# Attention in steps of a whole block: sixteen half groups of scores mixed with maxima, then the block's sixteen pairs of products, into one output bank

## The chip, the cores and the metric

The kernel runs on one core of one Trainium2 chip. The metric is the device time of one execution in microseconds (us), the median of several runs.

## What is computed

One transformer block with modulation, on x of 2 x 2048 x 576 in float32, 16 heads of 36 columns:

```python
ada = silu(c) @ W_ada + b_ada
shift_msa, scale_msa, gate_msa, shift_mlp, scale_mlp, gate_mlp = split(ada, 6)
h = modulate(layernorm(x), shift_msa, scale_msa)
x = x + gate_msa * attention(h, W_qkv, b_qkv, W_proj, b_proj)
h = modulate(layernorm(x), shift_mlp, scale_mlp)
x = x + gate_mlp * (gelu(h @ W_fc1 + b_fc1) @ W_fc2 + b_fc2)
# attention, for each of 2 x 16 (batch, head): softmax(q k^T / 6) v over 2048 keys, then @ W_proj
```

## The kernel before

The program has four stages one after the other: `phase_qkv`, `phase_attention`, `phase_proj`, `phase_mlp`. Each engine has its own instruction list, written out by hand, and the lists are tied together by semaphores; nothing reorders them. The change is in `phase_attention` and in the last chunk of `phase_qkv`.

**Attention.** There are 32 (batch, head) pairs, called heads here. For each head two things are computed from queries and keys.

- *Maxima.* TensorE multiplies 128 queries by 512 keys into one PSUM bank `sp` (`score_max`, L1024), and VectorE reduces the bank to the maximum of each row (L1083). A head has 64 of these units. When a head's 64 are there, VectorE takes the maxima of four (L1089), TensorE transposes the result (L1030), VectorE splits it into two parts `mh` and `ml` (L1095, L1097), and SyncE writes them as two further rows into the head's query tile, so that the scores of the next pass have the maximum already subtracted.
- *Probabilities and values.* For each half group x (128 keys by 512 queries) TensorE computes scores into one of three PSUM banks `st` (`scores_t`, L1042) and ScalarE takes the exponential into half of a tile `pt` (`exps`, L1132; 8 tiles). Two half groups make a group. For a group (`products`, L1053) TensorE multiplies both halves of the probabilities by the values, one to partitions 0 to 36 and one to partitions 64 to 100 of an output bank `op`; the trace has four matmul records for a group. Eight groups make a block (512 queries by all keys): their products accumulate in one bank. ScalarE then moves the two halves of the bank out (L1143 to `oa`, L1144 to `ob`), GpSimd adds them (L1197), SyncE stores the sum. There are 4 blocks in a head and 128 in all.

**The order.** `plan` is a list of 258 steps. Step b holds the 8 half groups 8b to 8b+7, 8 maxima units that run 72 ahead (`THERE = 72`: the first 72 are made in `phase_qkv`), and after them the products of the four groups of step b - 1. Within a step TensorE takes the units in turn: maximum, scores, maximum, scores, and so on; in place 2 there is no maximum, and the last maximum follows the last scores. A matmul to an `sp` bank waits until the bank's use three units earlier has been reduced (`slot_free`; three banks `sp`). A matmul of scores waits until the exponential three half groups earlier has been read (`s_p`, x - 2). There are two output banks `op`; the products of a block wait until the block before last has been moved out (`s_oa`).

ScalarE does, in a step, the 8 exponentials, and in every second step behind them both evictions of a finished block. So a step is a run of 16 matmuls for scores and maxima (called the score run below) and a run of products (the product run), in turn. Banks: 3 `st`, 2 `op`, 3 `sp`.

The last 9 steps with scores have no maxima left. From step `LAST` = 248 on, five steps also have a *turn*: one matmul into an `sp` bank (L1061), a VectorE product (L1123) and a ScalarE copy (L1152), for the stage behind. The projection's weights (`weight`, `W0`), the row sums (`INV`) and first tokens are loaded in between at given steps.

**The last chunk of `phase_qkv`.** TensorE computes nine feature tiles (14 matmuls each, L595), each evicted by ScalarE (L820, L821). `maxima(c, kind, n)` puts two maxima units of head 1 ahead of each of the last four tiles (L574, reduced at L744). Head 1's queries and keys are loaded before that (`second_loads`, L477).

Of the kernel before, what the change touches and what calls it, by code (L numbers as in the profile page):

```python
# [9 lines left out]
ALU = mybir.AluOpType  # L10
# [13 lines left out]
NCH = T // CH  # L24
# [265 lines left out]
def phase_qkv(nc, A, ident, adaT, eps, bq, sc, qs0, ks0, qs1, ks1, hh0, lo0, mx, nm, mh, ml, gd, xf, cond, W_ada,  # L290
# [96 lines left out]
    def maxima(c, kind, n):  # L387


        place = n + 4 if kind == "qk" else n  # L390
        k = 26 * (c - HCH) + 2 * place - 18
        if 0 <= k < 64:
            return range(k, k + 2)
        if c == NCH - 1 and place > 8:
            return range(64 + 2 * (place - 9), 66 + 2 * (place - 9))
        return range(0)

    def evacuated(e, n):
# [455 lines left out]
def phase_attention(nc, A, W, ident, qs0, ks0, qs1, ks1, mx, nm, mh, ml, gd, W_proj, b_proj, xf, qkh, qkl, vd, ot,  # L854
# [9 lines left out]
    NB = 3  # L864
    NP = 8
    G = NH * 32
    NBAT = G // 4
    NBLK = G // 8
    W0 = 24
    LAST = NBAT - 8  # L870
    INV = NBLK // 2 + 6
    THERE = 72
    qs = [qs0, qs1, A.sb("qs2", [128, L], R)]
    ks = [ks0, ks1, A.sb("ks2", [128, L], R)]
    vs = [A.sb(f"vs{i}", [128, 16, VW]) for i in range(2)]
# [2 lines left out]
    ob = [A.sb(f"ob{i}", [VW, 512]) for i in range(2)]  # L878
    oc = W.oc
    st = [A.ps(f"st{i}", [128, 512]) for i in range(3)]  # L880
    op = [A.ps(f"op{i}", [128, 512]) for i in range(2)]
    sp = [A.ps(f"sp{i}", [128, 512]) for i in range(3)]
    s_qk, s_m, s_v, s_o = A.sems("qk", NB), A.sems("m", NB), A.sems("v", 2), W.s_o
    s_one = A.sem("one")
    s_s, s_mx, s_nm, s_mt, s_mh = A.sem("s"), A.sem("mx"), A.sem("nm"), A.sem("mt"), A.sem("mh")
# [5 lines left out]

    plan, slots = [], []
    todo = THERE
    for b in range(NBAT + 2):
        s = Step()
        s.b, s.last = b, None
        s.late = plan[-1].last if plan else None
        s.slot = None
        if s.late is not None:
            s.slot = len(slots)  # L900
            slots.append(("mh", s.late))
        s.units = [[] for _ in range(9)]
        for i in range(min(8, NH * 64 - todo)):
            s.units[(0, 1, 3, 4, 5, 6, 7, 8)[i]].append((todo, len(slots)))
            slots.append(("mx", todo))
            todo += 1
            if todo % 64 == 0:
                s.last = todo // 64 - 1
        s.turn = s.turn_slot = None
        if LAST < b <= LAST + KT:  # L910
            s.turn, s.turn_slot = b - LAST - 1, len(slots)
            slots.append(("turn", s.turn))
        s.now = b - 1 if 0 < b <= NBAT else None
        s.block = (b - 3) // 2 if b > 2 and b % 2 else None
        plan.append(s)

    def slot_free(e, k):

        if k > 2:
            kind, n = slots[k - 3]  # L920
            if kind == "mx":
                e.wait_ge(s_mx, n - THERE + 1)
            elif kind == "turn":
                e.wait_ge(W.s_u, n + 1)
            else:
                e.wait_ge(s_mh, 2 * n)
# [8 lines left out]

    def weight(b):

        j, r = divmod(b - W0, 4)
        return divmod(j, KT) if 0 <= j < 2 * KT and r == 0 else (None, None)

    def sync(e):
# [28 lines left out]
        for s in plan:  # L970
            i, kt = weight(s.b)
            if i is not None:
                if i == 1 and kt < 2:
                    e.wait_ge(W.w[0].lo, KT)
                W.w[i].load(e, kt, W.stg, W_proj)
            if s.late is not None:
                max_rows(s.late)
            if s.b < NBAT:
                h, r = divmod(s.b, 8)
                if r == 0 and h + 2 < NH:  # L980
                    load(h + 2)
                if r == 2 and h + 1 < NH:
                    load_v(h + 1)
            if s.block is not None:
                h, u = divmod(s.block, 4)
                hd, i = h % H, s.block % 2
                cols = slice((h // H) * L + u * 512, (h // H) * L + u * 512 + 512)
                e.wait_ge(s_oc, s.block + 1)
                e.dma_start(ot[hd * D:hd * D + D, cols], oc[i][0:D, :]).then_inc(s_o[i], 16)
                e.dma_start(sm[hd:hd + 1, cols], oc[i][D:D + 1, :]).then_inc(s_o[i], 16)  # L990
                if s.block == INV - 4:
                    for i in range(2):
                        e.wait_ge(s_o[i], 32 * NBLK // 4)
                    W.load_sums(e, 0, sm)
                elif s.block == INV + 4:
                    for c in range(HCH):
                        W.place(e, 0, c)
            if s.b == LAST - 2:
                W.load_tokens(e, 0, W.oi, ot)
            elif s.b == LAST + 1:  # L1000
                e.wait_ge(W.s_sel, 5)
                W.load_x(e, 0, W.x1, xf)
# [15 lines left out]
    def tensor(e):  # L1018
        def score_max(n, slot):
            h, k = divmod(n, 64)  # L1020
            qb, k4, i = k // 4, k % 4, h % NB
            loaded(e, h)
            slot_free(e, slot)
            e.matmul(sp[slot % 3][:, :], qs[i][0:108, qb * 128:qb * 128 + 128], ks[i][0:108, k4 * 512:k4 * 512 + 512],  # L1024
                     start=True, stop=True).then_inc(s_s, 1)

        def max_rows(h, slot):
            e.wait_ge(s_nm, h)
            slot_free(e, slot)
            e.transpose(sp[slot % 3][0:16, 0:128], nm[:, :], ident[:, :]).then_inc(s_mt, 1)  # L1030

        def scores_t(x):
            h, u, kb = x // 64, (x // 16) % 4, x % 16
# [11 lines left out]
        def products(g):  # L1045
            h, blk, j = g // 32, g // 8, g % 8
            if g % 32 == 0:
                e.wait_ge(s_v[h % 2], 16 * (h // 2 + 1))
            if j == 0 and blk > 1:
                e.wait_ge(s_oa, 2 * (blk - 1))  # L1050
            e.wait_ge(s_p, 2 * g + 2)
            for a in range(2):
                ins = e.matmul(op[blk % 2][64 * a:64 * a + VW, :], vs[h % 2][:, 2 * j + a, :],  # L1053
                               pt[g % NP][:, a * 512:a * 512 + 512], start=j == 0, stop=j == 7)
            ins.then_inc(s_pv, 1)

        def turn(kt, slot):
            e.wait_ge(W.s_sel, 5)
            e.wait_ge(W.s_rr, 32 * HCH)
            slot_free(e, slot)  # L1060
            e.matmul(sp[slot % 3][:, :], W.sel[:, kt, :], W.rr[:, 0, :], start=True, stop=True).then_inc(W.s_ta, 1)  # L1061

        for s in plan:
            if s.late is not None:
                max_rows(s.late, s.slot)
            for q in range(9):
                for n, slot in s.units[q]:
                    score_max(n, slot)
                if q < 8 and s.b < NBAT:
                    scores_t(8 * s.b + q)  # L1070
            if s.turn is not None:
                turn(s.turn, s.turn_slot)
            if s.now is not None:
                for q in range(4):
                    products(4 * s.now + q)

    def vector(e):
        def score_max(n, slot):
            k = n % 64
            e.wait_ge(s_s, n - THERE + 1)  # L1080
            if k < 2:
                e.wait_ge(s_nm, n // 64 - 1)
            e.tensor_reduce(mx[:, k // 4, k % 4:k % 4 + 1], sp[slot % 3][:, :], AX.X, ALU.max).then_inc(s_mx, 1)  # L1083

        def row_max(h):
            e.wait_ge(s_mx, 64 * (h + 1) - THERE)
# [4 lines left out]
        def max_rows(h, slot):  # L1091
            e.wait_ge(s_mt, h)
            rows_there(e, h - 1)
            src = sp[slot % 3][0:16, 0:128]
            e.tensor_copy(mh[:, :], src).then_inc(s_mh, 1)  # L1095
            e.wait_ge(s_mh, 2 * h - 1)
            e.tensor_tensor(ml[:, :], src, mh[:, :].bitcast(F), ALU.subtract).then_inc(s_mh, 1)  # L1097
# [10 lines left out]
        for s in plan:  # L1108
            if s.late is not None:
                max_rows(s.late, s.slot)  # L1110
            for q in range(9):
                for n, slot in s.units[q]:
                    score_max(n, slot)
                    if n % 64 == 63:
                        row_max(n // 64)
            if s.block == INV:
                W.invert(e, 0)
            if s.b == LAST:
# [1 line left out]
            if s.turn is not None:  # L1120
                e.wait_ge(W.s_ta, s.turn + 1)
                e.wait_ge(W.s_a[0], 48)
                e.tensor_tensor(W.oi[:, s.turn, :], sp[s.turn_slot % 3][:, :], W.oi[:, s.turn, :], ALU.mult).then_inc(  # L1123
                    W.s_u, 1)

    def scalar(e):
        def exps(x):
# [3 lines left out]
                e.wait_ge(s_pv, g - NP + 1)  # L1131
            e.activation(pt[g % NP][:, a * 512:a * 512 + 512], st[x % 3][:, :], ACT.Exp, scale=SCALE).then_inc(s_p, 1)  # L1132

        for s in plan:
            if s.b < NBAT:
                for q in range(8):
                    exps(8 * s.b + q)
            if s.block is not None:
                i = s.block % 2
                e.wait_ge(s_pv, 8 * (s.block + 1))  # L1140
                if s.block > 1:
                    e.wait_ge(s_oc, s.block - 1)
                e.activation(oa[i][:, :], op[i][64:64 + VW, :], ACT.Copy).then_inc(s_oa, 1)  # L1143
                e.activation(ob[i][:, :], op[i][0:VW, :], ACT.Copy).then_inc(s_oa, 1)  # L1144
            if s.block == INV + 1:
                W.high(e, 0)
            i, kt = weight(s.b - 2)
# [702 lines left out]
```

## Time and profile before

| what | us |
|---|---|
| median of 3 runs | 3583.03 (3578.46 to 3584.28) |
| the profiled execution, its own time | 3576.74 |
| its span, first to last instruction | 3574.8 |
| attention, first matmul to end of the last | 458.37 to about 2443.7 |
| TensorE busy by the records | 3506.8 (98%) |
| VectorE busy | 1885.4 (53%) |
| ScalarE busy | 1557.3 (44%) |
| GpSimd busy | 360.5 (10%) |

The ends of matmul records are modelled, and records overlap, so 98% does not say that TensorE has no gaps; the starts of weight loads (rows of PEld) and of matmuls say more. PE is TensorE, PEld its weight loads, DVE VectorE, ACT ScalarE, POOL GpSimd, SPq the queue of SyncE. A row of the timeline merges instructions of one line: start, time from the first's start to the last's end, engine, line, operation, tiles, count, and in brackets the idle time before it with what ended it.

### The profile page before, as it was taken

The page shows a single profiled execution, that of the slowest core. Times are in us where ns is not written, and L with a number is a line of the kernel's source. Part 1 is how long each engine was busy: PE and PEld are TensorE (multiplying, and loading weights), DVE is VectorE, ACT ScalarE, POOL GpSimd, SP SyncE. Part 2 cuts the span into 40 slices and gives each one's busy share as a digit, 9 for nine tenths or more (in the row PEclk, how much of TensorE's full clock was granted, in tenths as well). Part 3 has the DMA queues.
Part 4 walks back from the last instruction along what each step waited for, and adds up shares of the span by engine and source line. Part 5 has one row for each costly group of instructions (what it writes and reads, how often), then busy time and mean ns, then how long its engine had stood idle before and what let it go on. Part 6 is the DMA issues. An engine that isn't in the chain of part 4 may idle for free. (4 is left out here: it accounts for less than half of the span.)

```text
span 3574.8 us, 46332 instructions
## 1 busy us (share of the span) xinstructions
PE 3506.8 (98%) x16996; PEld 2252.1 (63%) x16996; DVE 1885.4 (53%) x3415; ACT 1557.3 (44%) x2904; POOL 360.5 (10%) x284
## 2 busy tenths in 40 slices
PE   7999999999999999999999999999889999999999
PEld 5888844444444444444444444436779899898988
DVE  5446566666666666666666666634552322333232
ACT  3223256566655655565556555665550111211010
POOL 1000010111100000000000000014521010000000
PEclk9999999999999999999999999999999999999999
DMA  5554431211212111111212111114763132422221
GB/s 193 163 172 142 136 84 29 58 44 41 53 30 52 29 48 33 40 43 32 52 29 53 29 49 33 29 37 136 261 204 106 61 100 65 142 83 93 73 87 50
DMA packets 144672, 285.54 MB, mean 80 GB/s; under 512 B 18290, under 2 KB 44146, under 8 KB 137536
## 3 DMA queue, kind: packets, MB, share of 16 engines
q1 hardware_dynamic: 143236, 282.57, 25.8%
q8 instruction: 142, 2.33, 0.3%
q14 instruction: 78, 0.64, 0.1%
q10 hardware_dynamic: 1216, 0.00, 0.0%
HBM read 177.09 MB, written 104.34 MB: 79 GB/s over the span
## 5 line engine op out<-in xcount | busy, mean ns | idle before, releaser
L1083 DVE TENSOR_REDUCE q_mx<-b_sp 128x1 f32<-128x512 f32 x1976 | 1203.9, 681 | 614.1 <-PE b_sp L1024 614.1
L1132 ACT ACTIVATE b_pt<-b_st 128x512 f32<-128x512 f32 x2048 | 1030.9, 626 | 782.4 <-PE b_st L1042 782.3
L1053 PE MATMUL b_op<-b_pt,b_vs 128*37 128x512 f32 x4096 | 929.5, 596 | 0.0
L1053 PEld LDWEIGHTS b_op<-b_pt,b_vs 128*37 128x37 f32 x4096 | 223.8, 114 | 537.1 <-issue 458.1
L1805 ACT ACTIVATE d_af<-n_pf,q_mx 128x512 f32<-128x512 f32 x144 | 98.9, 687 | 730.3 <-PE n_pf L1728 729.5
L1745 PE MATMUL d_pm<-d_vl,d_ah 128*128 128x288 f32 x1152 | 339.9, 295 | 0.0
L1746 PE MATMUL d_pm<-d_vh,d_al 128*128 128x288 f32 x1152 | 339.8, 295 | 0.0
L1744 PE MATMUL d_pm<-d_vh,d_ah 128*128 128x288 f32 x1152 | 339.7, 295 | 0.0
L1197 POOL TENSOR_TENSOR w_oc<-b_oa,b_ob 37x512 f32<-37x512 f32 x128 | 161.3, 1260 | 1721.7 <-ACT b_ob L1144 1712.2
L1024 PE MATMUL b_sp<-q_hh,q_lo 108*128 108x512 f32 x696 | 295.6, 425 | 4.5 <-PEq L846 4.5
L1042 PE MATMUL b_st<-q_lo,q_hh 110*128 110x512 f32 x704 | 275.3, 414 | 1.8 <-ACT b_pt L1132 1.8
L1042 PE MATMUL b_st<-q_qs,q_ks 110*128 110x512 f32 x704 | 273.2, 409 | 0.2 <-ACT b_pt L1132 0.2
L1024 PE MATMUL b_sp<-q_ks,q_qs 108*128 108x512 f32 x640 | 271.7, 424 | 0.0
L1024 PE MATMUL b_sp<-b_ks,b_qs 108*128 108x512 f32 x640 | 270.2, 422 | 0.0
L1042 PE MATMUL b_st<-b_qs,b_ks 110*128 110x512 f32 x640 | 246.6, 406 | 0.0
L1744 PEld LDWEIGHTS d_pm<-d_vh,d_ah 128*128 128x128 f32 x1152 | 216.4, 188 | 0.7
L1745 PEld LDWEIGHTS d_pm<-d_vl,d_ah 128*128 128x128 f32 x1152 | 216.4, 188 | 0.7
L1746 PEld LDWEIGHTS d_pm<-d_vh,d_al 128*128 128x128 f32 x1152 | 216.4, 188 | 0.0
L1766 DVE CAST d_ah<-d_af 128x512 fp32r<-128x512 f32 x144 | 61.5, 427 | 280.3 <-ACT d_af L1805 280.3
L1024 PEld LDWEIGHTS b_sp<-q_hh,q_lo 108*128 108x128 f32 x696 | 131.7, 189 | 104.4 <-issue 88.3
L1779 DVE TENSOR_TENSOR d_ug<-d_pm,d_gt 128x288 f32<-128x288 f32 x128 | 58.5, 457 | 250.8 <-PE d_pm L1746 250.8
L1042 PEld LDWEIGHTS b_st<-q_lo,q_hh 110*128 110x128 f32 x704 | 131.9, 188 | 86.6 <-ACT b_pt L1132 67.9
(299 smaller groups left out, 4599.7 us busy)
## 6 DMA issues: line engine op xcount, KB each, us to landing
qkh<-a_th SPq DMA_DIRECT2D x72, 256.0 KB, 2.0
qkl<-a_tl SPq DMA_DIRECT2D x72, 256.0 KB, 2.2
d_yi<-y SPq DMA_DIRECT2D x64, 288.0 KB, 3.0
vd<-a_vx SPq DMA_DIRECT2D x8, 1184.0 KB, 6.2
b_vs<-vd SPq DMA_DIRECT2D x32, 296.0 KB, 2.8
a_x<-in_x SPq DMA_DIRECT2D x8, 1152.0 KB, 6.7
ot<-w_oc SPq DMA_DIRECT2D x128, 72.0 KB
y<-d_yi SPq DMA_DIRECT2D x32, 288.0 KB, 2.2
```

The costliest lines, as they stand in the source:

```text
L1024: e.matmul(sp[slot % 3][:, :], qs[i][0:108, qb * 128:qb * 128 + 128], ks[i][0:108, k4 * 512:k4 * 512 + 512], start=True, stop=True).then_i ...
L1042: e.matmul(st[x % 3][:, :], ks[i][0:110, kb * 128:kb * 128 + 128], qs[i][0:110, u * 512:u * 512 + 512], start=True, stop=True).then_inc(s_ ...
L1053: ins = e.matmul(op[blk % 2][64 * a:64 * a + VW, :], vs[h % 2][:, 2 * j + a, :], pt[g % NP][:, a * 512:a * 512 + 512], start=j == 0, stop= ...
L1083: e.tensor_reduce(mx[:, k // 4, k % 4:k % 4 + 1], sp[slot % 3][:, :], AX.X, ALU.max).then_inc(s_mx, 1)
L1132: e.activation(pt[g % NP][:, a * 512:a * 512 + 512], st[x % 3][:, :], ACT.Exp, scale=SCALE).then_inc(s_p, 1)
L1197: e.tensor_tensor(oc[i][:, :], oa[i][:, :], ob[i][:, :], ALU.add).then_inc(s_oc, 1)
L1744: e.matmul(out, ah[:, f, ts], vh[:, f, cs], start=f == 0, stop=False)
L1745: e.matmul(out, ah[:, f, ts], vl[:, f, cs], start=False, stop=False)
L1746: ins = e.matmul(out, al[:, f, ts], vh[:, f, cs], start=False, stop=f == NT - 1)
L1766: e.tensor_copy(ah[:, f, :], af[m % 2][:, :]).then_inc(s_ah, 1)
L1779: e.tensor_tensor(ug[m % 2][:, :], pm[m % 4][:, 0:HALF], gt[:, b, cs], ALU.mult).then_inc(s_ug, 1)
L1805: e.activation(af[m % 2][:, :], pf[m % 4][:, :], ACT.Gelu_apprx_tanh, bias=b1[:, half * NT + f:half * NT + f + 1]).then_inc(s_af, 1)
```

## The change

Steps become whole blocks. For the first 124 blocks (`LAST = NBLK - 4`) step b holds the 16 half groups of block b, each scores matmul directly behind a maximum (16 maxima while there are any), and then the products of the same block's 8 groups. There are four banks `sp` and one bank `op`: a use of an `sp` bank waits for the use four units earlier, and a block's first product waits until the block before it has been moved out. ScalarE moves out the half at partition 64 at the start of the next step, ahead of its first exponential, and the other half behind that step's exponential 12 (counted from 0). The last four blocks go in steps of 8 half groups with the products of the 4 groups before, one step later than their scores; in these steps both evictions stand ahead of the exponentials. 80 maxima units instead of 72 are made in `phase_qkv`: two ahead of each of the last eight feature tiles. The loads, the weights and the turn keep about their places.

```diff
@@ phase_qkv, maxima
-        if c == NCH - 1 and place > 8:
-            return range(64 + 2 * (place - 9), 66 + 2 * (place - 9))
+        if c == NCH - 1 and place > 4:
+            return range(64 + 2 * (place - 5), 66 + 2 * (place - 5))
@@ phase_attention
-    NBAT = G // 4
     NBLK = G // 8
-    W0 = 24
-    LAST = NBAT - 8
+    W0 = 12
+    LAST = NBLK - 4
     INV = NBLK // 2 + 6
-    THERE = 72
+    THERE = 80
...
-    op = [A.ps(f"op{i}", [128, 512]) for i in range(2)]
-    sp = [A.ps(f"sp{i}", [128, 512]) for i in range(3)]
+    op = A.ps("op", [128, 512])
+    sp = [A.ps(f"sp{i}", [128, 512]) for i in range(4)]
...
-    for b in range(NBAT + 2):
+    for b in range(NBLK + 6):
         s = Step()
-        s.b, s.last = b, None
+        s.b, k = b, b - LAST
         s.late = plan[-1].last if plan else None
-        s.slot = None
+        s.slot = s.last = s.turn = s.turn_slot = None
...
-        s.units = [[] for _ in range(9)]
-        for i in range(min(8, NH * 64 - todo)):
-            s.units[(0, 1, 3, 4, 5, 6, 7, 8)[i]].append((todo, len(slots)))
-            slots.append(("mx", todo))
-            todo += 1
-            if todo % 64 == 0:
-                s.last = todo // 64 - 1
-        s.turn = s.turn_slot = None
-        if LAST < b <= LAST + KT:
-            s.turn, s.turn_slot = b - LAST - 1, len(slots)
+        if k < 0:
+            s.halves, s.groups, s.block = range(16 * b, 16 * b + 16), range(8 * b, 8 * b + 8), b - 1 if b else None
+        else:
+            x = 16 * LAST + 8 * k
+            s.halves = range(x, min(x + 8, 2 * G))
+            s.groups = range(x // 2 - 4, min(x // 2, G)) if k else range(0)
+            s.block = LAST - 1 + k // 2 if k == 0 or k > 2 and k % 2 else None
+        s.units = []
+        for x in s.halves:
+            if todo < NH * 64:
+                s.units.append((todo, len(slots)))
+                slots.append(("mx", todo))
+                todo += 1
+                if todo % 64 == 0:
+                    s.last = todo // 64 - 1
+        if 0 < k <= KT:
+            s.turn, s.turn_slot = k - 1, len(slots)
             slots.append(("turn", s.turn))
-        s.now = b - 1 if 0 < b <= NBAT else None
-        s.block = (b - 3) // 2 if b > 2 and b % 2 else None
...
-        if k > 2:
-            kind, n = slots[k - 3]
+        if k > 3:
+            kind, n = slots[k - 4]
...
-        j, r = divmod(b - W0, 4)
+        j, r = divmod(b - W0, 2)
@@ sync
-            if s.b < NBAT:
-                h, r = divmod(s.b, 8)
+            if s.b < LAST:
+                h, r = divmod(s.b, 4)
                 if r == 0 and h + 2 < NH:
                     load(h + 2)
-                if r == 2 and h + 1 < NH:
+                if r == 1:
                     load_v(h + 1)
@@ tensor
-            if j == 0 and blk > 1:
-                e.wait_ge(s_oa, 2 * (blk - 1))
+            if j == 0 and blk:
+                e.wait_ge(s_oa, 2 * blk)
             e.wait_ge(s_p, 2 * g + 2)
             for a in range(2):
-                ins = e.matmul(op[blk % 2][64 * a:64 * a + VW, :], vs[h % 2][:, 2 * j + a, :],
+                ins = e.matmul(op[64 * a:64 * a + VW, :], vs[h % 2][:, 2 * j + a, :],
...
-            for q in range(9):
-                for n, slot in s.units[q]:
+            for q, x in enumerate(s.halves):
+                for n, slot in s.units[q:q + 1]:
                     score_max(n, slot)
-                if q < 8 and s.b < NBAT:
-                    scores_t(8 * s.b + q)
+                scores_t(x)
             if s.turn is not None:
                 turn(s.turn, s.turn_slot)
-            if s.now is not None:
-                for q in range(4):
-                    products(4 * s.now + q)
+            for g in s.groups:
+                products(g)
@@ scalar
+        def evict(block, half):
+            i = block % 2
+            e.wait_ge(s_pv, 8 * (block + 1))
+            if block > 1:
+                e.wait_ge(s_oc, block - 1)
+            to, r = ((oa[i], 64), (ob[i], 0))[half]
+            e.activation(to[:, :], op[r:r + VW, :], ACT.Copy).then_inc(s_oa, 1)
+
         for s in plan:
-            if s.b < NBAT:
-                for q in range(8):
-                    exps(8 * s.b + q)
             if s.block is not None:
-                i = s.block % 2
-                e.wait_ge(s_pv, 8 * (s.block + 1))
-                if s.block > 1:
-                    e.wait_ge(s_oc, s.block - 1)
-                e.activation(oa[i][:, :], op[i][64:64 + VW, :], ACT.Copy).then_inc(s_oa, 1)
-                e.activation(ob[i][:, :], op[i][0:VW, :], ACT.Copy).then_inc(s_oa, 1)
+                evict(s.block, 0)
+                if s.b >= LAST:
+                    evict(s.block, 1)
+            for q, x in enumerate(s.halves):
+                exps(x)
+                if q == 12 and s.block is not None:
+                    evict(s.block, 1)
```

## Rows read from the trace of the kernel before

**Rows 1.** The profile's page: span and clock, and busy time by engine
```profile
span 3574.8 us, 46332 instructions
PE 3506.8 (98%) x16996; PEld 2252.1 (63%) x16996; DVE 1885.4 (53%) x3415; ACT 1557.3 (44%) x2904; POOL 360.5 (10%) x284
...
PEclk9999999999999999999999999999999999999999
```
**Rows 2.** Busy time in stretches: us, PE, PEld, DVE, ACT, POOL, PEclk, DMA share, GB/s
```profile
480.00:1000.00 520.00, 520.00 (x2154) 242.13 (x2154) 332.19 (x560) 315.55 (x614) 70.64 (x54) 1.00 0.17 43
...
2000.00:2360.00 360.00, 360.00 (x1491) 167.63 (x1488) 229.27 (x387) 213.22 (x416) 28.98 (x23) 1.00 0.14 36
```
**Rows 3.** Timeline of one usual step and the next step's start
```profile
1519.80 0.49 PE L1024 MATMUL b_sp<-q_ks,q_qs 108*128 108x512 f32 x1
...
1520.33 4.88 DVE L1083 TENSOR_REDUCE q_mx<-b_sp 128x1 f32<-128x512 f32 x8 [2.85 <-PE b_sp L1024]
...
1520.57 4.03 ACT L1132 ACTIVATE b_pt<-b_st 128x512 f32<-128x512 f32 x8 [3.71 <-PE b_st L1042]
...
1523.53 0.19 PEld L1024 LDWEIGHTS b_sp<-q_ks,q_qs 108*128 108x128 f32 x1 [0.17 <-issue]
...
1523.96 0.15 PEld L1053 LDWEIGHTS b_op<-b_pt,b_vs 128*37 128x37 f32 x4 [0.25 <-issue]
...
1527.53 0.50 PE L1024 MATMUL b_sp<-q_ks,q_qs 108*128 108x512 f32 x1
```
**Rows 4.** Timeline, the two steps that open attention
```profile
458.37 0.47 PE L1024 MATMUL b_sp<-q_hh,q_lo 108*128 108x512 f32 x1 [4.55 <-PEq L846]
...
461.86 7.92 DVE L1083 TENSOR_REDUCE q_mx<-b_sp 128x1 f32<-128x512 f32 x13 [0.16 <-PE b_sp L1024]
...
468.05 0.19 PEld L1024 LDWEIGHTS b_sp<-q_hh,q_lo 108*128 108x128 f32 x1 [0.30 <-DVE q_mx L1083]
468.48 0.15 PEld L1053 LDWEIGHTS b_op<-b_pt,b_vs 128*37 128x37 f32 x4 [0.24 <-issue]
```
**Rows 5.** Timeline, a step with the transposed maxima, and the next one's start
```profile
1504.07 0.28 PE L1030 MATMUL b_sp<-g_ident,q_nm 128*16 128x128 f32 x1
...
1512.07 0.50 PE L1024 MATMUL b_sp<-q_ks,q_qs 108*128 108x512 f32 x1
```
**Rows 6.** Timeline, the steps without maxima and the end of attention
```profile
2373.86 0.28 PE L1030 MATMUL b_sp<-g_ident,q_nm 128*16 128x128 f32 x1
...
2381.01 0.96 PE L1042 MATMUL b_st<-q_lo,q_hh 110*128 110x512 f32 x3
2381.55 4.03 ACT L1132 ACTIVATE b_pt<-b_st 128x512 f32<-128x512 f32 x8 [1.88 <-PE b_st L1042]
...
2384.59 3.63 PE L1053 MATMUL b_op<-b_pt,b_vs 128*37 128x512 f32 x16
2388.15 0.96 PE L1042 MATMUL b_st<-q_lo,q_hh 110*128 110x512 f32 x3
...
2391.72 0.49 PE L1061 MATMUL b_sp<-w_rr,w_sel 48*128 48x512 f32 x1
2392.15 3.63 PE L1053 MATMUL b_op<-b_pt,b_vs 128*37 128x512 f32 x16
...
2436.66 7.07 PE L1053 MATMUL b_op<-b_pt,b_vs 128*37 128x512 f32 x32
...
2443.77 0.59 ACT L1143 ACTIVATE b_oa<-b_op 37x512 f32<-37x512 f32 x1 [4.89 <-PE b_op L1053]
2444.39 0.59 ACT L1144 ACTIVATE b_ob<-b_op 37x512 f32<-37x512 f32 x1
```
**Rows 7.** Timeline of the last chunk of the first stage, evictions of four tiles
```profile
435.62 0.69 ACT L820 ACTIVATE a_tf<-a_pm,g_bq 128x512 f32<-128x512 f32 x1 [2.01 <-PE a_pm L595]
...
438.90 0.69 ACT L820 ACTIVATE a_tf<-a_pm,g_bq 128x512 f32<-128x512 f32 x1 [2.01 <-PE a_pm L595]
...
442.64 0.69 ACT L820 ACTIVATE a_tf<-a_pm,g_bq 128x512 f32<-128x512 f32 x1 [2.48 <-PE a_pm L595]
...
446.39 0.69 ACT L820 ACTIVATE a_tf<-a_pm,g_bq 128x512 f32<-128x512 f32 x1 [2.48 <-PE a_pm L595]
```
**Rows 8.** Timeline of SyncE's queue, the last load of head 1
```profile
412.92 0.37 SPq L477 DMA_DIRECT2D q_hh<-qkl  x1
```
**Rows 9.** Busy time in stretches of the same chunk, columns as in rows 2
```profile
410.00:414.00 4.00, 4.00 (x31) 3.91 (x30) 2.29 (x5) 0.00 (x0) 0.00 (x0) 1.00 0.63 185
414.00:418.00 4.00, 4.00 (x32) 4.00 (x32) 1.04 (x3) 0.00 (x0) 0.00 (x0) 1.00 0.76 197
418.00:422.00 4.00, 4.00 (x32) 3.96 (x32) 0.92 (x2) 0.00 (x0) 0.00 (x0) 1.00 0.53 135
422.00:426.00 4.00, 4.00 (x20) 3.31 (x19) 0.92 (x3) 0.22 (x1) 0.00 (x0) 1.00 0.51 156
```

More of the change, by code:

```diff
@@ L1023, in score_max @@
             slot_free(e, slot)
-            e.matmul(sp[slot % 3][:, :], qs[i][0:108, qb * 128:qb * 128 + 128], ks[i][0:108, k4 * 512:k4 * 512 + 512],
+            e.matmul(sp[slot % 4][:, :], qs[i][0:108, qb * 128:qb * 128 + 128], ks[i][0:108, k4 * 512:k4 * 512 + 512],
                      start=True, stop=True).then_inc(s_s, 1)
@@ L1029, in max_rows @@
             slot_free(e, slot)
-            e.transpose(sp[slot % 3][0:16, 0:128], nm[:, :], ident[:, :]).then_inc(s_mt, 1)
+            e.transpose(sp[slot % 4][0:16, 0:128], nm[:, :], ident[:, :]).then_inc(s_mt, 1)
         def scores_t(x):
@@ L1060, in turn @@
             slot_free(e, slot)
-            e.matmul(sp[slot % 3][:, :], W.sel[:, kt, :], W.rr[:, 0, :], start=True, stop=True).then_inc(W.s_ta, 1)
+            e.matmul(sp[slot % 4][:, :], W.sel[:, kt, :], W.rr[:, 0, :], start=True, stop=True).then_inc(W.s_ta, 1)
         for s in plan:
@@ L1082, in score_max @@
                 e.wait_ge(s_nm, n // 64 - 1)
-            e.tensor_reduce(mx[:, k // 4, k % 4:k % 4 + 1], sp[slot % 3][:, :], AX.X, ALU.max).then_inc(s_mx, 1)
+            e.tensor_reduce(mx[:, k // 4, k % 4:k % 4 + 1], sp[slot % 4][:, :], AX.X, ALU.max).then_inc(s_mx, 1)
         def row_max(h):
@@ L1093, in max_rows @@
             rows_there(e, h - 1)
-            src = sp[slot % 3][0:16, 0:128]
+            src = sp[slot % 4][0:16, 0:128]
             e.tensor_copy(mh[:, :], src).then_inc(s_mh, 1)
@@ L1110, in vector @@
                 max_rows(s.late, s.slot)
[L1111 to L1115, printed above, removed]
+            for n, slot in s.units:
+                score_max(n, slot)
+                if n % 64 == 63:
+                    row_max(n // 64)
             if s.block == INV:
@@ L1122, in vector @@
                 e.wait_ge(W.s_a[0], 48)
-                e.tensor_tensor(W.oi[:, s.turn, :], sp[s.turn_slot % 3][:, :], W.oi[:, s.turn, :], ALU.mult).then_inc(
+                e.tensor_tensor(W.oi[:, s.turn, :], sp[s.turn_slot % 4][:, :], W.oi[:, s.turn, :], ALU.mult).then_inc(
                     W.s_u, 1)
```

## The prediction, made before the changed kernel ran

> **What bounds the kernel now.** I read the page first: TensorE is busy 98% of the span at the full clock, VectorE 53%, ScalarE 44% [rows 1], and the stretches say the same of attention alone, with VectorE at 64% [rows 2]. So TensorE is the engine to follow, but its records overlap, and small waits hide in them. The timeline of one step shows these waits. A step takes 1527.53 - 1519.80 = 7.73 us: a score run of 4.16 (to the first product at 1523.96) and a product run of 3.57 [rows 3]. The score run has 16 matmuls. A full 512-column matmul takes 0.235 us where nothing waits: two more of them lengthen a feature tile's step in the first stage from 3.28 to 3.74 us [rows 7], 0.23 each. So 16 would take 3.76. The other 0.40 are two things: the last maximum's weight load at 1523.53 has waited for a reduction, and behind it the first product's weight load comes 0.43 later instead of 0.235 (0.25 idle) [rows 3]. Call the latter the switch. Reductions come every (4.88 - 0.68) / 7 = 0.600 us, the first 0.53 after the run's start, so the fifth ends at 0.53 + 5 x 0.600 = 3.53, and the eighth maximum's load, which needs its bank, stands at 3.73: 0.20 later. The run's end is thus set by VectorE and the three banks, though only some 0.2 us worse than TensorE alone.
>
> **The main loop.** In the new run of 16 units maximum 15 (from 0) needs the bank of maximum 11, so twelve reductions must have ended: 0.53 + 12 x 0.600 + 0.20 = 7.93. One scores matmul stands behind it now, 0.235, and then the switch of 0.43: the first product starts at 8.60. TensorE alone would be there at 32 x 0.235 + 0.20 = 7.72. The old kernel passes two runs of eight in 8.32, since the product run between them lets VectorE empty its three banks and start again with all free; the fourth bank gives back only one of these two refills. The nearest row for a long run is the opening of attention, 16 maxima in a row: 13 reductions in 7.92 us, a pitch of 0.603, and near its end each maximum's load is held (0.30 idle, released by the reduction) [rows 4]. That is the pattern that I expect in every block.
>
> The product run of 8 groups: at the end of attention 32 records take 7.07 against 3.63 for 16 [rows 6], 3.44 more, so 3.57 + 3.44 = 7.01. The pause at a product run's end, about 0.13, is thus paid once in a block instead of twice.
>
> A block: 8.60 + 7.01 = 15.61, against 15.46 for two steps. The step with the transposed maxima takes 8.00 instead of 7.73 [rows 5] and keeps its 0.27: the transposition holds VectorE's first reduction up by the same time once in a head.
>
> Blocks 0 to 122 have 16 maxima each. Block 0 opens like the two steps of before, 10.11 to the first product [rows 4], less one reduction (fourth bank), plus one matmul: 9.75, then 7.01. The sum is 16.76 + 122 x 15.61 + 30 x 0.27 = 1929.3. Before, steps 0 to 246 took 2373.86 - 458.37 = 1915.5. So **+13.8**.
>
> **The end of attention.** Without maxima ScalarE sets the run: the first exponential stands 0.54 after the start, the pitch is (4.03 - 0.60) / 7 = 0.49, scores 7 need five of them, and the first product stands 0.59 after that: 3.58 as shown, 7.14 for a step [rows 6]. A single eviction ahead of the exponentials lets the first start at 0.10 + 0.62 = 0.72, two at 1.34 (the last pair of evictions starts as the last products end and is 0.62 apart) [rows 6]. Block 123: 0.72 + 13 x 0.49 + 0.59 = 7.68, and 7.01: 14.7. The first two half steps have no products between them: 1.34 + 6.37 + 0.59 = 8.3, a turn of 0.43 (2392.15 - 2391.72), products 3.56: 12.3. Six steps of 7.14, four turns, and three steps that now begin with two evictions, 0.80 more each: 47.0. Last products 3.5. Together 77.5, against 2443.73 - 2373.86 = 69.9 [rows 6]: **+7.6**. Some 7 of it is not new work: the products of one step have moved from the first sum to this one, and the first had one step more.
>
> **The first stage** gets 8 maxima more: four tiles x 0.46 = **+1.8** [rows 7]. Do head 1's rows arrive in time? The last load is issued at 412.92 [rows 8]. The first of these maxima would start four tiles before the first one of before, near 425.6. The queues move 185, 197 and 135 GB/s in the three stretches of 4 us from 410 to 422, 2.1 MB [rows 9], more than the six loads of 0.29 MB. Nothing is lost, unless they land over 3 us later than that.
>
> **What costs nothing, and its cover.** The eviction at a step's start ends its pitch at 0.72, and the first exponential can't start before 0.77 (1520.57 - 1519.80) [rows 3]; if it is later by 0.1, the exponentials still run 0.9 ahead of the reductions at unit 15, which is their cover. The eviction behind exponential 12: scores 12 start at 8.27 - 3 x 0.60 = 6.47, the exponential at 6.91, the eviction at 7.40, its end at 8.02, and the product that needs the bank stands at 8.60. GpSimd, the stores on SyncE and the transposed rows wait behind it, but have 8 us to spare; the rows now come a whole block ahead of use. Weight loads and value loads keep their lead. ScalarE's work per block is 16 x 0.49 + 2 x 0.62 = 9.1 us of 15.6.
>
> **The sum**: 13.8 + 7.6 + 1.8 = +23.2 us on the profiled execution's own 3576.74, so 3600. The median of the runs shown is 6.3 higher, 3583.03; I predict against it: **3606**.
>
> **Rule and row.** The rows show 0.25 us of idle weight loading each time TensorE goes from scores to products, and the matmuls there have 37 columns in two halves of the array. The Trainium skill, "TensorEngine Tiling (Array Packing)", Key Properties, says that a change of tiling mode, as opposed to a change of tile, drains TensorE. By that rule alone the change gains, as the switches are halved: about 0.20 + 0.13 for each of 124 blocks, 41 us, and the time would be 3542. My sum has this gain in it (one switch and one pause in a block instead of two); it is eaten by VectorE's hold.
>
> **Rivals.**
> *Faster: reductions do not hold the run.* Then TensorE ends the run at 7.72, and so does ScalarE (0.77 + 13 x 0.49 + 0.59 = 7.73): 0.88 less than in my sum, 123 times, -108 us, 3498. It decides if the pitch of reductions falls under 0.588, at which the block is even. For it: VectorE is idle 2.85 us in each step [rows 3], its average load of 64% leaves room. Against it: this idle time lies in the product run, where no maxima come; and the pitch is 0.600 to 0.603 in both runs shown. Gains smaller than this one come from a shorter release or switch.
> *No change.* The main loop's excess is a difference of two large numbers, 0.15 us; if the release is 0.16 as in the opening [rows 4], and the scores matmul behind the last maximum is half hidden, it falls to about 0, and the other terms leave +5: 3588. That is within 0.2%, 7 us, about what a measurement of this kernel can tell from no change.
> *Slower still: the single output bank.* If the eviction behind exponential 12 comes over 0.58 later than I place it, products wait. With it behind all the exponentials it would end at 8.02 + 3 x 0.49 = 9.5, 0.9 after the product's time: 0.9 x 122 = +110, 3716. The Trainium skill, "Perfetto Trace Analysis", Optimization Strategy, says that a gap repeated on the engine that should be full can mean too few PSUM buffers. The old rows can't show this wait for one bank.
> *Late rows of head 1*: some us once.
>
> **Chances.** My forecast, 3592 to 3619, has 0.72; slower with the output bank's wait in part or whole 0.07; between +0.2% and 3592 0.03; no change 0.08; faster 0.10, most of it by a smaller cost of switches than by the full rival. So faster 0.10, same 0.08, slower 0.82. The range, 3587 to 3620, takes in the bounds of the release (0.16 to 0.23, with 0.235 more or less half hidden) and of the pitch (0.600 to 0.603).
>
> **What would show it.** In the profile after: reductions in groups of 16 with a pitch of 0.600 and an idle time near 5 us between groups; maxima's weight loads held by reductions from about unit 9 on, 0.3 us each; blocks 15.6 us apart; product runs of 7.0; no weight load of a product that waits for L1144's successor; two evictions and then the exponentials in the last steps. Wrong it would be if the block is 15.3 or less, or if weight loads of products wait for evictions.

## The result and the profile after

The changed kernel takes 3603.55 us in the median (3600.18 to 3603.82, 4 runs) against 3582.28 (3578.46 to 3584.28, 4 runs): a ratio of 1.0062, 95% interval 1.0049 to 1.0075. It is slower by 21 us, and 3606 was predicted. The profiled execution took 3603.8.

The page's head, which answers to [rows 1]:

```profile
span 3602.1 us, 46459 instructions
PE 3531.1 (98%) x16996; PEld 2250.7 (62%) x16996; DVE 1874.5 (52%) x3415; ACT 1563.4 (43%) x2904; POOL 362.6 (10%) x284
```

TensorE's share still reads 98%. The span gained 27.3 us, and TensorE's busy time 24.3 (3531.1 against 3506.8 of [rows 1]) with the same 16996 matmuls: its records have grown over the waits, so no idle time shows there. The weight loads in the timeline show these waits. This is one usual block, from its first weight load to the next block's; it answers to [rows 3]:

```profile
1541.65 0.19 PEld L1028 LDWEIGHTS b_sp<-q_ks,q_qs 108*128 108x128 f32 x1 [0.83 <-issue]
1541.77 0.60 ACT L1141 ACTIVATE b_oa<-b_op 37x512 f32<-37x512 f32 x1 [6.29 <-PE b_op L1057]
1542.19 9.66 DVE L1085 TENSOR_REDUCE q_mx<-b_sp 128x1 f32<-128x512 f32 x16 [5.91 <-PE b_sp L1028]
1542.42 6.72 ACT L1133 ACTIVATE b_pt<-b_st 128x512 f32<-128x512 f32 x13
...
1548.97 0.19 PEld L1028 LDWEIGHTS b_sp<-q_ks,q_qs 108*128 108x128 f32 x1 [0.30 <-issue]
1549.04 0.58 ACT L1141 ACTIVATE b_ob<-b_op 37x512 f32<-37x512 f32 x1
1549.08 0.19 PEld L1046 LDWEIGHTS b_st<-b_qs,b_ks 110*128 110x128 f32 x1
1549.57 0.19 PEld L1028 LDWEIGHTS b_sp<-q_ks,q_qs 108*128 108x128 f32 x1 [0.30 <-issue]
1549.68 0.19 PEld L1046 LDWEIGHTS b_st<-b_qs,b_ks 110*128 110x128 f32 x1
1550.22 0.15 PEld L1057 LDWEIGHTS b_op<-b_pt,b_vs 128*37 128x37 f32 x4 [0.35 <-issue]
1550.22 7.07 PE L1057 MATMUL b_op<-b_pt,b_vs 128*37 128x512 f32 x32
...
1557.22 0.19 PEld L1028 LDWEIGHTS b_sp<-q_ks,q_qs 108*128 108x128 f32 x1 [0.83 <-issue]
```

The block takes 1557.22 - 1541.65 = 15.57 us. The first product stands 8.57 after the start, the product run takes 7.00. The 16 reductions have a pitch of (9.66 - 0.68) / 15 = 0.599, and the loads of the last maxima stand 0.60 apart with 0.30 idle ahead of each: VectorE's pitch has become TensorE's. The profile puts this idle time down to "issue" and names no releaser, so that it is a wait for reductions is read from the equal pitch, and shown by the experiments with banks and columns below. The last maximum's load is at 7.92, and one scores matmul and the switch follow it, 0.65. The first eviction is over before the first exponential; the second ends at 1549.62, 0.6 before the product that needs the bank.

The difference, stage by stage in the profiled executions. Attention begins at 460.82 instead of 458.37 (+2.4). From there to the step with the last transposed maxima it takes 2386.37 - 460.82 = 1925.6 instead of 1915.5 (+10.1). From that step to the last product it takes 79.8 instead of 69.9 (+9.9). The stages behind attention take 1136.0 instead of 1131.1 (+4.9). The four add up to the 27.3 of the span. Between the medians it is 21.3, since the profiled execution of before lay 5.5 below its median and the one of the changed kernel at its median.

This is the end of attention, TensorE's timeline, from the two merged score runs on; it answers to [rows 6]:

```profile
2401.05 0.96 PE L1046 MATMUL b_st<-q_lo,q_hh 110*128 110x512 f32 x3
2402.91 6.65 PE L1046 MATMUL b_st<-q_lo,q_hh 110*128 110x512 f32 x13 [0.90 <-ACT b_pt L1133]
2409.49 0.79 PE L1065 MATMUL b_sp<-w_rr,w_sel 48*128 48x512 f32 x1
2410.22 6.07 PE L1057 MATMUL b_op<-b_pt,b_vs 128*37 128x512 f32 x16
2416.22 0.97 PE L1046 MATMUL b_st<-q_lo,q_hh 110*128 110x512 f32 x3
2417.40 2.45 PE L1046 MATMUL b_st<-q_lo,q_hh 110*128 110x512 f32 x5 [0.22 <-ACT b_pt L1133]
```

The 16 product records take 6.07 instead of the 3.63 of [rows 6]. The stretches give the reason: PEclk, the granted clock, is the first number behind the five busy times of a row.

```profile
2394.00:2401.00 7.00, 7.00 (x33) 1.83 (x32) 0.00 (x0) 1.39 (x3) 1.27 (x1) 1.00 0.05 13
2401.00:2406.00 5.00, 4.10 (x12) 1.95 (x10) 0.00 (x0) 4.80 (x10) 1.27 (x1) 0.89 0.17 28
2406.00:2410.20 4.20, 4.20 (x9) 2.09 (x8) 0.00 (x0) 4.20 (x9) 0.00 (x0) 0.50 0.74 266
2410.20:2416.20 6.00, 6.00 (x17) 1.27 (x16) 0.69 (x1) 0.63 (x1) 2.64 (x2) 0.59 0.00 0
2416.20:2424.00 7.80, 7.58 (x28) 2.70 (x27) 0.69 (x1) 4.77 (x10) 0.00 (x0) 1.00 0.00 1
```

TensorE ran at its lower level, 1.2 GHz, from 2406 into the product run, after a score run in which it waited 0.90 us for the two evictions ahead of the exponentials and then gave one matmul in each 0.49 us. These 2.4 us were not in the prediction.

The 4.9 us behind attention are the clock too. These are the first 20 us behind the last product, in the changed kernel and in the one before:

```profile
2466.00:2486.00 20.00, 15.58 (x62) 13.05 (x60) 4.46 (x10) 3.08 (x5) 4.67 (x4) 0.66 0.68 201
...
2444.00:2464.00 20.00, 15.86 (x91) 13.56 (x92) 7.37 (x13) 3.48 (x6) 6.37 (x5) 0.91 0.68 201
```

The granted clock is 0.66 instead of 0.91, and TensorE gives 62 matmuls instead of 91. From the first one of the next stage to VectorE's first RECIPROCAL there it takes 2488.57 - 2470.57 = 18.00 instead of 2461.94 - 2448.14 = 13.80, so 4.2 of the 4.9 arise there. Why the clock came back later in this execution is open.

### The profile page after: what moved, and what is told of

Read it like the earlier page. It is cut to its first block and busy times, and to the rows that moved or that the text cites. A ratio compares the mean times of both kernels' runs of the same rounds, so it can differ in the third digit from the quotient of the medians.

```text
span 3602.1 us, 46459 instructions
## 1 busy us (share of the span) xinstructions
PE 3531.1 (98%) x16996; PEld 2250.7 (62%) x16996; DVE 1874.5 (52%) x3415; ACT 1563.4 (43%) x2904; POOL 362.6 (10%) x284
## 5 line engine op out<-in xcount | busy, mean ns | idle before, releaser
L1085 DVE TENSOR_REDUCE q_mx<-b_sp 128x1 f32<-128x512 f32 x1968 | 1187.6, 676 | 545.3 <-PE b_sp L1028 545.3
L1133 ACT ACTIVATE b_pt<-b_st 128x512 f32<-128x512 f32 x2048 | 1063.2, 616 | 20.2 <-PE b_st L1046 11.6
L1057 PE MATMUL b_op<-b_pt,b_vs 128*37 128x512 f32 x4096 | 907.3, 595 | 0.0
L1057 PEld LDWEIGHTS b_op<-b_pt,b_vs 128*37 128x37 f32 x4096 | 234.8, 114 | 601.0 <-issue 561.8
L1141 ACT ACTIVATE b_oa<-b_op 37x512 f32<-37x512 f32 x128 | 76.3, 596 | 785.9 <-PE b_op L1057 785.9
L1046 PE MATMUL b_st<-q_qs,q_ks 110*128 110x512 f32 x704 | 281.0, 400 | 0.4 <-ACT b_pt L1133 0.4
L1028 PE MATMUL b_sp<-q_ks,q_qs 108*128 108x512 f32 x640 | 279.7, 437 | 0.0
L1028 PE MATMUL b_sp<-b_ks,b_qs 108*128 108x512 f32 x640 | 279.6, 437 | 0.0
L1028 PEld LDWEIGHTS b_sp<-b_ks,b_qs 108*128 108x128 f32 x640 | 120.3, 188 | 132.2 <-issue 120.0
```

Of the source, the lines that this page charges most:

```text
L1028: e.matmul(sp[slot % 4][:, :], qs[i][0:108, qb * 128:qb * 128 + 128], ks[i][0:108, k4 * 512:k4 * 512 + 512], start=True, stop=True).then_i ...
L1046: e.matmul(st[x % 3][:, :], ks[i][0:110, kb * 128:kb * 128 + 128], qs[i][0:110, u * 512:u * 512 + 512], start=True, stop=True).then_inc(s_ ...
L1057: ins = e.matmul(op[64 * a:64 * a + VW, :], vs[h % 2][:, 2 * j + a, :], pt[g % NP][:, a * 512:a * 512 + 512], start=j == 0, stop=j == 7)
L1085: e.tensor_reduce(mx[:, k // 4, k % 4:k % 4 + 1], sp[slot % 4][:, :], AX.X, ALU.max).then_inc(s_mx, 1)
L1141: e.activation(to[:, :], op[r:r + VW, :], ACT.Copy).then_inc(s_oa, 1)
```

## The experiments

The theory: the score run ends when reductions have freed the last maximum's bank, so its length goes with the units in a run less the banks, at 0.60 us each. The rivals: the switches, the output bank, or TensorE's own work.

**The last pair turned round.** In whole-block steps the last scores stand ahead of the last maximum.

```diff
             for q, x in enumerate(s.halves):
+                if q == 15:
+                    scores_t(x)
                 for n, slot in s.units[q:q + 1]:
                     score_max(n, slot)
-                scores_t(x)
+                if q < 15:
+                    scores_t(x)
```

> In whole-block steps the scores 15 stand ahead of maximum 15 instead of behind it. Theory (the score run ends when twelve reductions have freed the last maximum's bank, and what stands behind that maximum is exposed): the wait is filled with the scores matmul, first product 0.43 after the last maximum's weight load instead of 0.65, block 15.57 - 0.22 = 15.35, 123 blocks: -27 us against the changed kernel, about 3577. Rival (TensorE's own work or the output bank sets the run): no change, 3604.

Measured 3585.79 us (10 runs), 1.0014 of before (1.0005 to 1.0024): -18 us against the changed kernel, not -27. The end of its score run, weight loads:

```profile
1525.04 0.19 PEld L1028 LDWEIGHTS b_sp<-q_ks,q_qs 108*128 108x128 f32 x1 [0.30 <-issue]
1525.15 0.42 PEld L1046 LDWEIGHTS b_st<-b_qs,b_ks 110*128 110x128 f32 x2
1525.64 0.19 PEld L1028 LDWEIGHTS b_sp<-q_ks,q_qs 108*128 108x128 f32 x1
1526.16 0.15 PEld L1057 LDWEIGHTS b_op<-b_pt,b_vs 128*37 128x37 f32 x4 [0.33 <-issue]
```

The last maximum's load is not held any more, and the product comes 0.52 behind it, where I had expected 0.43. I had taken the whole matmul, 0.235, as hidden. But between two releases, 0.60 apart, TensorE has two matmuls of its own to do, 0.47, so only 0.13 is free, and 0.13 is what came out: reductions stand 15.43 apart from block to block (1533.69 - 1518.26) against 15.57. 0.13 x 123 = 16 us, and attention up to the last transposed maxima is 15.8 shorter (2370.72 - 460.99 = 1909.7 against 1925.6). The rest of the 18 is not the swap's: in the profiled executions the end of attention took 84.8 instead of 79.8, with four product runs at a lower clock instead of one, and the stages behind it 1128.3 instead of 1136.0. The direction is the theory's, the rival that expected nothing falls, and my price was wrong by a term that the rows of before already held.

**Three banks for maxima**, one output bank as in the change.

```diff
-    sp = [A.ps(f"sp{i}", [128, 512]) for i in range(4)]
+    sp = [A.ps(f"sp{i}", [128, 512]) for i in range(3)]
...
-        if k > 3:
-            kind, n = slots[k - 4]
+        if k > 2:
+            kind, n = slots[k - 3]
```

> Three banks for maxima instead of four, one output bank as in the change. Theory: maximum 15 waits for thirteen reductions instead of twelve, +0.60 in each block with maxima, block 16.17, +74 us, about 3678. Rival (the run is set by ScalarE, the switch or the output bank): up to +15 us.

Measured 3676.98 (1 run). VectorE's timeline:

```profile
1502.86 9.66 DVE L1085 TENSOR_REDUCE q_mx<-b_sp 128x1 f32<-128x512 f32 x16 [6.51 <-PE b_sp L1028]
1519.03 9.65 DVE L1085 TENSOR_REDUCE q_mx<-b_sp 128x1 f32<-128x512 f32 x16 [6.51 <-PE b_sp L1028]
```

The block is 16.17, as expected, 0.60 more. One bank is one reduction, to the hundredth.

**Quicker reductions, in both kernels.** The reduction reads 448 of the 512 columns; the kernels leave 64 columns out of each maximum.

```diff
-            e.tensor_reduce(mx[:, k // 4, k % 4:k % 4 + 1], sp[slot % 4][:, :], AX.X, ALU.max).then_inc(s_mx, 1)
+            e.tensor_reduce(mx[:, k // 4, k % 4:k % 4 + 1], sp[slot % 4][:, 0:448], AX.X, ALU.max).then_inc(s_mx, 1)
```

> The changed kernel with reductions over 448 of the 512 columns (leaves 64 columns out of each maximum). A reduction's pitch should fall by 64 columns at 0.96 per ns, from 0.600 to about 0.53. Theory: the hold goes, the run falls from 8.57 to about 7.75 where ScalarE (0.77 + 13 x 0.49 + 0.59) and TensorE (7.72) take over, block 14.76, -99 us against the changed kernel, about 3505. Rival (the hold is not the reductions): less than -20 us.

> The kernel before with reductions over 448 of the 512 columns (leaves 64 columns out of each maximum). Theory: its score run of 8 was held by only 0.2 us, so it falls from 4.16 to about 3.96, -0.20 in each of 247 steps, -49 us, about 3533: so with quick reductions the changed kernel would win by some 28 us, which is the gain of half the switches less the slower end of attention. Rival (long runs gain nothing at any pitch): before stays ahead of the changed kernel with this edit too.

Measured 3508.21 for the changed kernel and 3538.74 for the one before, 1 run each: -95 and, against the runs of before beside them (3580.77), -42. Reductions of the changed kernel, VectorE's timeline:

```profile
1531.40 8.59 DVE L1085 TENSOR_REDUCE q_mx<-b_sp 128x1 f32<-128x448 f32 x16 [2.94 <-PE b_sp L1028]
1546.17 4.34 DVE L1085 TENSOR_REDUCE q_mx<-b_sp 128x1 f32<-128x448 f32 x8 [6.18 <-PE b_sp L1028]
```

The block falls to 14.77, and no load of a maximum near its end waits 0.30. So the order of the two kernels turns round: with an eighth less work in each reduction the changed one is 30 us ahead. The gain of longer runs is real, and it is VectorE's hold that eats it. Before's step fell to 7.60 (1507.98 - 1500.38), by 0.13 and not 0.20: the last scores matmul now waits for ScalarE (0.19 idle ahead of its load), and it and the maximum behind it end the run at 4.03. At the end of the changed kernel's run the profile names the output bank:

```profile
1508.02 0.62 ACT L1141 ACTIVATE b_ob<-b_op 37x512 f32<-37x512 f32 x1
...
1508.80 0.15 PEld L1057 LDWEIGHTS b_op<-b_pt,b_vs 128*37 128x37 f32 x4 [0.29 <-ACT b_ob L1141]
```

The run ends at 7.8, and the second eviction is the last releaser that the profile finds. But it holds nothing up. The eviction is over 0.16 before the product, and where a product does wait for it, in the experiment below, it follows by 0.05. The product stands 0.32 behind the start of the last scores matmul (1508.80 - 1508.48), as in the changed kernel with all columns (1550.22 - 1549.90), where the bank had long been free.

**The second eviction late.**

```diff
-                if q == 12 and s.block is not None:
+                if q == 15 and s.block is not None:
                     evict(s.block, 1)
```

> In the changed kernel the second eviction of the output bank stands behind all 16 exponentials instead of behind exponential 12. Theory (the single bank costs nothing as placed, since the eviction ends 0.6 us before the product that needs the bank): now it starts after exponential 15, whose scores end the run; exponential 15 starts near 8.70 after the run's start, the eviction at 9.19, its end with release near 9.9, against 8.57 for the product: +1.3 us in each of 123 blocks, about +160, 3764. Rival (the product does not wait for the bank, or the wait is already in the changed kernel): under +60.

Measured 3752.67 (1 run). Weight loads:

```profile
1517.78 0.15 PEld L1057 LDWEIGHTS b_op<-b_pt,b_vs 128*37 128x37 f32 x4 [1.60 <-ACT b_ob L1141]
```

The product waits 1.60 instead of 0.35, +1.25 in a block, and 149 us in all. The single bank is thus free of charge only because of where the eviction stands, and the rival of the prediction had its mechanism and its sign right; the change avoids it by somewhat less than 0.6 us.

**Whole blocks to the end.** No half steps; turns in blocks 123 to 127.

```diff
-    LAST = NBLK - 4
+    LAST = NBLK - 6
...
-    for b in range(NBLK + 6):
+    for b in range(NBLK + 1):
...
+        s.block = b - 1 if b else None
-        if k < 0:
-            s.halves, s.groups, s.block = range(16 * b, 16 * b + 16), range(8 * b, 8 * b + 8), b - 1 if b else None
-        else:
...
+        s.halves, s.groups = range(16 * b, min(16 * b + 16, 2 * G)), range(8 * b, min(8 * b + 8, G))
...
-                if s.b >= LAST:
+                if s.b == NBLK:
```

> The changed kernel with whole-block steps to the end: no half steps for the last four blocks, turns in blocks 123 to 127. Theory: the half steps and their two leading evictions took 79.8 us from step 123 on, 2.4 of it at the halved clock of TensorE; five whole blocks without maxima take 5 x 14.7 + 5 turns of 0.43 = 75.6: -4 us, about 3600, and the first product run behind two merged score runs is not slow any more. Rival (the end of attention is set elsewhere, the clock falls anyway): no change or +2.

Measured 3604.27 (4 runs), 1.0063 of before (1.0049 to 1.0077): no gain on the changed kernel. TensorE's stretches and product runs in its last blocks:

```profile
2375.00:2390.00 15.00, 14.58 (x59) 5.64 (x57) 9.51 (x20) 8.67 (x18) 1.27 (x1) 1.00 0.02 7
2390.00:2405.00 15.00, 15.00 (x47) 5.33 (x46) 0.69 (x1) 7.79 (x16) 1.26 (x1) 0.77 0.26 85
2405.00:2420.00 15.00, 14.57 (x43) 5.22 (x44) 0.69 (x1) 9.03 (x18) 3.88 (x3) 0.77 0.02 6
```

```profile
2405.66 6.68 PE L1041 MATMUL b_st<-q_lo,q_hh 110*128 110x512 f32 x13 [0.43 <-ACT b_pt L1128]
2412.99 8.30 PE L1052 MATMUL b_op<-b_pt,b_vs 128*37 128x512 f32 x32
```

My theory of this part fell. The five product runs there take 8.19 to 8.39 instead of 7.07: behind each score run of 16 without maxima, in which TensorE gives a matmul in 0.49 us, the product run begins at the lower level of the clock. That is no fixed rule, though. The same score run of 16 in the changed kernel's block 123 left the clock at 1.00 (7.06 for the products, the row 2394.00:2401.00 above). And runs of 8 can be hit: none of the product runs at the end of attention is slow in the kernel before [rows 6], but two are in the steps of 8 below (5.33 instead of 3.63 each). What the profiles share is that the first product run behind two merged score runs was slow in all five that have one (4.72 to 6.23 us). Attention's end takes 2472.39 - 2387.44 = 85.0 us here, 5.2 more than in the changed kernel, though the whole time is the same, as the stages behind took 1130.0, with the clock back early (0.91 in the first 20 us).

**Steps of 8 with four banks and one output bank.** If units less banks is what counts, the kernel before should take the fourth bank and keep its short steps.

```diff
-    op = [A.ps(f"op{i}", [128, 512]) for i in range(2)]
-    sp = [A.ps(f"sp{i}", [128, 512]) for i in range(3)]
+    op = A.ps("op", [128, 512])
+    sp = [A.ps(f"sp{i}", [128, 512]) for i in range(4)]
...
-            s.units[(0, 1, 3, 4, 5, 6, 7, 8)[i]].append((todo, len(slots)))
+            s.units[i].append((todo, len(slots)))
...
-            if j == 0 and blk > 1:
-                e.wait_ge(s_oa, 2 * (blk - 1))
+            if j == 0 and blk:
+                e.wait_ge(s_oa, 2 * blk)
...
+            if s.block is not None:
+                evict(s.block, 0)
+            for q in range(8 if s.b < NBAT else 0):
+                exps(8 * s.b + q)
+                if q == 4 and s.block is not None:
+                    evict(s.block, 1)
```

> The kernel before, steps of 8 half groups, with four banks for maxima and one output bank (evictions: one ahead of the exponentials, one behind exponential 4), and each maximum straight ahead of its scores. Theory (it is the number of units per run over the number of banks that decides, not the number of switches): maximum 7 needs only four reductions, 0.54 + 2.40 + 0.20 = 3.14, so TensorE alone sets the run, 3.96 instead of 4.16, or 3.82 by ScalarE; step 7.53 instead of 7.73, -0.20 in 247 steps, -49 us, about 3533. If the eviction behind exponential 4 (end and release near 3.9) is late by 0.1, 3545. Rival (fewer switches are what pays, one output bank costs): no gain over before, 3581 or more.

Measured 3523.49 (5 runs), 0.9839 of before (0.9826 to 0.9853): 60 us faster than before and 80 faster than the change. One step, with an eviction in it:

```profile
1517.63 0.19 PEld L1024 LDWEIGHTS b_sp<-q_ks,q_qs 108*128 108x128 f32 x1 [0.83 <-issue]
1518.16 4.87 DVE L1083 TENSOR_REDUCE q_mx<-b_sp 128x1 f32<-128x512 f32 x8 [2.63 <-PE b_sp L1024]
...
1520.80 0.59 ACT L1140 ACTIVATE b_ob<-b_op 37x512 f32<-37x512 f32 x1
...
1521.57 0.15 PEld L1053 LDWEIGHTS b_op<-b_pt,b_vs 128*37 128x37 f32 x4 [0.37 <-ACT b_ob L1140]
...
1525.66 4.87 DVE L1083 TENSOR_REDUCE q_mx<-b_sp 128x1 f32<-128x512 f32 x8 [2.63 <-PE b_sp L1024]
```

The step is 1525.66 - 1518.16 = 7.50, and the product stands 3.94 after the start. That is the 3.96 of TensorE alone: weight loads in this run stand 0.235 apart from first to last. The releaser named is the eviction, but the next step, without one, has its product 3.94 after the start as well.

**The order of a pair.** Two kernels split that gain: before with only the paired order (the edit of `s.units` above), and the steps of 8 with all edits but that one.

> The kernel before with one edit: each maximum straight ahead of its scores, so that the last maximum stands ahead of the last scores (three banks for maxima, two output banks as before). Theory (with three banks maximum 7 needs five reductions and its load stands at 3.73; what follows it is exposed): first product at 3.73 + 0.65 = 4.38 instead of 4.16, +0.22 in each of 247 steps, +54 us, about 3637. Rival (the order of a pair is what made the steps of 8 with four banks fast): this kernel is faster than before.

> The steps of 8 with four banks for maxima and one output bank, but with the old order (no maximum in place 2, the last maximum behind the last scores). Theory: no reduction is waited for; ScalarE releases the last scores at 3.37, and they and the maximum behind them end the run near 4.04, as in the kernel before with reductions over 448 columns: step 7.60, -0.13 in 247 steps against before, -32 us, about 3550, so 27 slower than with the paired order. Rival (all of the gain is the fourth bank): as the paired order, 3523.

Measured 3640.03 (1 run) and 3542.84 (4 runs, 0.9895 of before, 0.9878 to 0.9912). Before with the paired order has steps of 7.95 (1507.48 - 1499.53), as expected: the order costs 0.22 where the last maximum is held. With four banks it is not held, and the old order has steps of 7.61 (1513.98 - 1506.37) against 7.50, as its last scores wait for ScalarE. So the fourth bank, taken from the output banks, brings some 36 us against the runs beside it (3578.52), and the paired order 19 to 24 more, but only with the fourth bank.

## Why the prediction was right

- *The score run.* Predicted 8.60 to the first product, measured 8.57; the last maximum's load 7.93 and 7.92; twelve reductions at 0.600 and 0.599. Three banks and 448 columns confirm the formula from both sides.
- *The product run.* 7.01 and 7.00. What one switch and one pause fewer are worth in a block, 0.20 + 0.13 in the prediction, can be bounded: two unheld steps of 8 in the same paired order, 2 x 7.50, against 14.77 with 448 columns differ by 0.23. Two steps of 7.60 against 14.77 give 0.43, but 0.2 of that is the old order's wait for ScalarE. The Trainium skill, "TensorEngine Tiling (Array Packing)", Key Properties, says that changing the tiling mode drains TensorE; that a drain is what a switch consists of, no run here shows.
- *The block.* 15.61 and 15.57. The 122 blocks behind the first one are 5 us too high in my sum, and the opening is 0.4 too low, 10.12 to the first product instead of 9.75: the first matmuls of attention ran at the lower clock for longer. So +10.1 where +13.8 stood.
- *The end of attention.* +9.9 where +7.6 stood. The missing term is the clock: the merged score run lowered it, and the product run behind took 2.4 longer. Without it the sum is right to 0.1, in part by luck: the turn and the last scores ahead of that product run cost 0.4 more at the lower clock, and a pair of evictions at a step's start costs 0.64 and not 0.80, three times.
- *The first stage.* A feature tile with two maxima has a pitch of 3.74 in the new places too, so +1.8 is right for these; attention begins 2.4 later, the rest of it lay ahead of this chunk. Head 1's rows were there in time: the new maxima start at 426.20, and the tiles keep their pitch.
- *The sum.* 13.8 + 7.6 + 1.8 = 23.2 against 22.4 for the same three in the profiled executions, and 21.3 between the medians. The 4.9 of the stages behind is not in the prediction. These stages took 1128.1 to 1131.1 in the nine profiles in which the clock was at 0.91 behind attention, four of them with whole-block steps, and 1136.0 and 1137.4 in the two at 0.66, so I do not count it as the change's. That 3606 lies so near 3603.55 is partly luck. For the profiled execution I had 3600, 3.9 too low; and I added 6.3 for the median, but this time the median did not lie above the profiled execution. The two errors cancel.
- *The rivals.* "Reductions do not hold the run" was given 3498, and the kernel with 448 columns, in which they do not, took 3508. The late eviction was priced at +110 and cost +149: I had let exponential 15 follow at its pitch, though its scores come only at the run's end.
- One step in it was loose: "the scores matmul behind the last maximum, 0.235" is right for what stands behind it, but is no measure of what is gained by moving it, as the first experiment showed.

## What to carry to other kernels

When two engines take turns on a ring of banks, look at the run's length less the number of banks, at the pitch of the slower one, and not at the share of busy time: here VectorE at 64% held TensorE. Merging short runs gives one start and one switch less, but the slower engine catches up once less, so price both from rows. Here two runs of 8 on three banks waited for ten reductions, one run of 16 on four banks for twelve: +1.20. Against it stood 1.16 for one start, release and switch, less 0.235 for the scores matmul now behind the last maximum, and 0.13 for one pause: some 0.15 lost by the sum, 0.11 measured (15.57 against 15.46). And before buying longer runs with a freed bank, try that bank in the short ones: with the paired order, that was worth 60 us.

## What the runs showed of the hardware that I had not expected

- TensorE's granted clock fell to its lower level, 1.2 GHz (0.50 in a stretch), inside attention, in stretches where it gave one 512-column matmul in 0.49 us. It fell so in every block without maxima of the kernel with whole blocks to the end (0.77 over 15 us, product runs of 8.19 to 8.39 instead of 7.07), but not each time in others. In the usual blocks, with two matmuls in 0.60 us while the reductions hold them, it stayed at 1.00.
- How long the clock stays low behind a pause is not the same in each execution: behind attention it was 0.66 over 20 us in two profiles and 0.91 in the nine others, and that was worth 5 to 9 us of the whole time.
- Records of reductions last 0.68 us while their pitch is 0.599, so a run of them must be counted by starts. The saving of 64 of 512 columns was (9.66 - 8.59) / 15 = 0.071 us each.
